# Attention's value products in two bursts of eight per head, with eight exponential buffers

## What is computed

```python
scores = einsum('bhqd,bhkd->bhqk', q, k) * scale          # 16 heads of 16 features
sparsity = scores.max(-1) - scores.mean(-1)
_, top_idx = top_k(sparsity, U)                             # U = 307 queries of 2048 per head
q_sel = take_along_axis(q, top_idx[..., None], axis=2)
attn = softmax(einsum('bhud,bhkd->bhuk', q_sel, k) * scale)
out_sel = einsum('bhuk,bhkd->bhud', attn, v)
out = zeros_like(q).at[bi, hi, top_idx].set(out_sel)
```

## Time and profile before

| what | us |
|---|---|
| median of 3 runs | 1661.31 (1660.96 to 1672.83) |
| the profiled execution's own time | 1666.39 |
| its span | 1664.6 |
| PE busy in the span | 1508.7 (91%) |
| DVE busy | 1225.6 (74%) |
| ACT busy | 1043.5 (63%) |
| granted TensorE clock, mean | 0.979 |

### The profile page before, as it was taken

How to read it: one execution, slowest core, us unless ns; L and a number is a source line. 1 busy time by engine, 2 the same in 40 slices (tenths; PEclk the granted TensorE clock), 3 DMA queues, 4 the chain that set the end, 5 groups by cost and what they waited for, 6 DMA issues and landing times.

```text
span 1664.6 us, 28574 instructions
## 1 busy us (share of the span) xinstructions
PE 1508.7 (91%) x8669; PEld 843.6 (51%) x8674; DVE 1225.6 (74%) x2906; ACT 1043.5 (63%) x1401; POOL 274.9 (17%) x321
## 2 busy tenths in 40 slices
PE   6799999998889979999998889989899999989999
PEld 3342222223445532222222645544698987479988
DVE  5569999998887749999999887856755452665511
ACT  4478888887756658888887446663333473333364
POOL 2340000001623343000000313341111000011100
PEclk9899999999999999999999999999999999999999
DMA  4662111211521121111112211111043402004410
GB/s 158 208 193 53 41 38 38 53 51 49 161 87 52 51 60 38 38 46 49 38 38 89 63 34 49 53 52 36 17 142 122 139 29 76 0 26 161 161 48 32
DMA packets 93336, 119.31 MB, mean 72 GB/s; under 512 B 22754, under 2 KB 78658, under 8 KB 92740
## 3 DMA queue, kind: packets, MB, share of 16 engines
q1 hardware_dynamic: 90180, 117.60, 23.3%
q0 software_dynamic: 3072, 0.66, 0.4%
HBM read 93.41 MB, written 24.78 MB: 71 GB/s over the span
## 4 chain that ended last, share of the span: by engine, by line
PE 45%; DVE 34%; issue 13%; DMA 4%; ACT 3%; SPq 1%; POOL 0%; DVEq 0%; ACTq 0%
DVE work_area L1208 24%; PE psum L2070 6%; PE psum L2008 6%; PE psum L1855 5%; PE psum L1876 5%; PE psum L1867 4%; PE psum L1951 4%; PE psum L2019 3%; DVE big_area L1208 2%; PE psum L2028 2%; DMA work_area<-heads_out 2%; PE psum L1691 2%; PE psum L2060 1%; PE psum L1716 1%; ACT big_area L891 1%
## 5 line engine op out<-in xcount | busy, mean ns | idle before, releaser
L1208 DVE CUSTOM_DVE_ANT_0 work_area<-psum,work_area 128x1024 f32<-128x1024 f32 x512 | 589.0, 1220 | 7.9 <-PE psum L1752 4.3
L820 ACT ACTIVATE work_area<-psum 128x1024 f32<-128x1024 f32 x512 | 511.0, 1027 | 75.7 <-DVE big_area L1208 30.1
L1752 PE MATMUL psum<-work_area 96*128 96x512 bf16 x1024 | 309.3, 384 | 47.9 <-DVE big_area L1208 6.8
L1742 PE MATMUL psum<-work_area 96*128 96x512 bf16 x1024 | 305.5, 380 | 7.4 <-ACT work_area L820 1.5
L838 ACT ACTIVATE work_area<-psum 128x614 f32<-128x614 f32 x256 | 164.1, 681 | 90.3 <-PE psum L1867 90.1
L1752 PEld LDWEIGHTS psum<-work_area 96*128 96x128 bf16 x1024 | 63.4, 97 | 266.3 <-DVE big_area L1208 251.2
L1742 PEld LDWEIGHTS psum<-work_area 96*128 96x128 bf16 x1024 | 88.8, 98 | 152.9 <-ACT work_area L820 59.0
L674 POOL DMA_INDIRECT heads_out<-work_area x96 | 98.3, 1024 | 193.8 <-DVE work_area L1374 172.7
L1352 DVE TENSOR_SCALAR big_area<-iota,rank 128x308 bf16<-128x308 f16 x512 | 119.0, 309 | 0.1
L2008 PE MATMUL psum<-work_area,xn 128*128 128x128 f32 x1024 | 118.5, 277 | 0.0
L2008 PEld LDWEIGHTS psum<-work_area,xn 128*128 128x128 f32 x1024 | 117.2, 194 | 0.2
(11 more groups left out here) (252 smaller groups left out, 1973.4 us busy)
## 6 DMA issues: line engine op xcount, KB each, us to landing
work_area<-in_L_ffn_w_dram SPq DMA_DIRECT2D x32, 1024.0 KB, 5.4
work_area<-k_parts SPq DMA_DIRECT2D x192, 64.2 KB, 2.2
work_area<-q_parts SPq DMA_DIRECT2D x192, 64.0 KB, 2.1
k_parts<-work_area SPq DMA_DIRECT2D x24, 384.0 KB, 4.1
q_parts<-work_area SPq DMA_DIRECT2D x16, 384.0 KB, 3.3
big_area<-q_parts SPq DMA_DIRECT2D x16, 384.0 KB, 5.5
work_area<-k_parts SPq DMA_DIRECT2D x32, 192.0 KB
x_res<-in_L_attn_x_dram SPq DMA_DIRECT2D x8, 512.0 KB, 5.7
```

The costliest lines, as they stand in the source:

```text
L820: s.activation(SC[:, t % 4], PS[:, 2 * (n % 2):2 * (n % 2) + 2].rearrange("p a n -> p (a n)"), ACT.Relu).then_inc(relu_done, 1)
L1208: v.tensor_tensor_reduce(SC[:, t % 4], PS[:, 4 + 2 * (t % 2):6 + 2 * (t % 2)].rearrange("p a n -> p (a n)"), SC[:, t % 4], 1.0, -3.0e38, A ...
L1742: last = mm(PS[:, 2 * (n % 2) + k], QS1[par][0:TERMS, t * P:(t + 1) * P], KS[par][0:TERMS, k * 512:(k + 1) * 512], start=True, stop=True)
L1752: last = mm(PS[:, 4 + 2 * (t % 2) + k], QS1[par][0:TERMS, t * P:(t + 1) * P], KS[par][0:TERMS, K1 + k * 512:K1 + (k + 1) * 512], start=Tru ...
```

## The change

PX grows from four to eight buffers (one for each pair of key tiles), five in the work area and three in EO. The two that overlap the busy area are now the last two, 6 and 7. The value products come in two bursts of eight key tiles. `pe_head` has a new order: scores 2, 3; the last 8 gathers of head h+1; rows(h); scores 4, 5; values 0; scores 6, 7; the first 8 gathers of head h+2; turn(h-1); then `k2_used`; scores 0, 1 of head h+1; values 1. Head 0 has all 16 gathers of head 1 after values 0, and head 1 has all 16 of head 2 after scores 2, 3. On ACT the copy of the next queries moves from behind exponential 6 to behind exponential 3 (head 0: behind 5), the wait for `parts_ready` moves ahead of exponential 6, and a wait for `zero_out` is added. DVE's order is unchanged; take_out waits for two bursts in place of four.

```diff
         OS = a.take([CH * P])
         QS = a.take([2, UP], BF16)
         SK = a.take([2, NT, TERMS + 6], BF16)
-        PX = a.take([4, 2, UP])
+        PX = [a.take([2, UP]) for _ in range(3)]
         OR = a.take([CH, DH + 1])
         ORr = a.take([CH])
         ON = a.take([2, CH, DH])
         IDX = a.take([2, CH], U32)
+        PX += [a.take([2, UP]) for _ in range(2)]
         attention_end = a.at
+        EO = sb("expert_out", [P, E, D])
+        zeros = EO[:].rearrange("p e d -> p (e d)")
+        a = Area(zeros)
+        for k in range(3):
+            PX.insert(3 + k, a.take([2, UP]))
         a = Area(work, L // 2)
         MK = a.take([2, NT * H], BF16)
...
         E2 = a.take([2, M])
         E2T = a.take([2, E, P])
         Y = a.take([2, D])
-        EO = sb("expert_out", [P, E, D])
-        zeros = EO[:].rearrange("p e d -> p (e d)")
         cmc = sb("slot_max_col", [P, E])
         warm = sb("exp_warm", [P, 1])
         nrm, z2, rz2 = (sb(n, [P, NT]) for n in ("nrm", "z2", "rz2"))
...
                     for k in gs:
                         v = i * 16 + (par * 8 + k)
                         act.wait_ge(s_ready, b * 128 + v + 1)
-                        act.wait_ge(p_used, b * 64 + i * 8 + (par * 4 + k // 2 + 1))
-                        slot = k % 4
-                        s.activation(PX[:, slot, :, 0:U], PS[:, 2 * (k % 2):2 * (k % 2) + 2, 0:U], ACT.Exp, scale=SCALE).then_inc(p_ready, 1)
-
+                        act.wait_ge(p_used, b * 32 + i * 4 + par * 2 + k // 4 + 1)
+                        s.activation(PX[k][:, :, 0:U], PS[:, 2 * (k % 2):2 * (k % 2) + 2, 0:U], ACT.Exp, scale=SCALE).then_inc(p_ready, 1)
+
+                act.wait_ge(zero_out, 64)
                 take_queries(0, 0, 0)
                 if b == 0:
                     second_part(1, NU - 1)
                 def act_head(i, par, more):
-                    if b == 0 and i == 0 and par == 0:
-                        exps(i, par, range(0, 3))
-                        act.wait_ge(parts_ready, B * NU)
-                    exps(i, par, range(3 if b == 0 and i == 0 and par == 0 else 0, 7))
+                    first = i == 0 and par == 0
+                    exps(i, par, range(0, 6 if first else 4))
                     if more:
                         take_queries(i, 1 - par, par + 1)
-                    exps(i, par, range(7, 8))
+                    if first and b == 0:
+                        act.wait_ge(parts_ready, B * NU)
+                    exps(i, par, range(6 if first else 4, 8))
                 for h in range(H):
                     act_head(h // 2, h % 2, h < H - 1)
...
                     v.tensor_scalar(IDX[:, par], PS[:, 7, CH * P:CH * P + CH], hcol[:, bass.ds(i * 2 + n, 1)], None, ALU.add).then_inc(idx_used, 1)
                 def take_out(i, par):
-                    dve.wait_ge(p_used, b * 64 + i * 8 + ((par + 1) * 4 + 2))
+                    dve.wait_ge(p_used, b * 32 + i * 4 + (par * 2 + 4))
                     v.tensor_copy(OS[:, 0:U], PS[:, 6 - par, 0:U]).then_inc(os_ready, 1)
                 def finish(i, par, n):
...
                         last = mm(PS[:, 2 * (k % 2) + kk, 0:U], K2S[n % 2][0:TERMS + 3, kt * P:(kt + 1) * P], QS[0:TERMS + 3, n % 2, 0:U], start=True, stop=True)
                     last.then_inc(s_ready, 1)
-                def values(i, n, k4):
-                    if k4 == 0:
+                def values(i, n, half):
+                    if half == 0:
                         pe.wait_ge(oT_used, max(0, b * H + i * 2 + n - 1))
-                    pe.wait_ge(p_ready, b * 128 + i * 16 + (n * 8 + 2 * k4 + 4))
-                    for q in range(4):
-                        kt = 4 * k4 + q
-                        last = mm(PS[32 * q:32 * q + DH + 1, 6 - n % 2, 0:U], V[:, kt, i * 2 + n], PX[:, kt // 2 % 4, kt % 2, 0:U], start=(kt < 4), stop=(kt >= NT - 4), skip_group_check=True)
+                    pe.wait_ge(p_ready, b * 128 + i * 16 + (n * 8 + 4 * half + 6))
+                    for kt in range(half * (NT // 2), (half + 1) * (NT // 2)):
+                        at = 32 * (kt % 4)
+                        last = mm(PS[at:at + DH + 1, 6 - n % 2, 0:U], V[:, kt, i * 2 + n], PX[kt // 2][:, kt % 2, 0:U], start=(kt < 4), stop=(kt >= NT - 4), skip_group_check=True)
                     last.then_inc(p_used, 1)
                 def rows(i, n):
...
                     last.then_inc(oT_ready, 1)
-                def pe_head(i, n, first, later):
-                    CUTS = (0, 0, NT // 2, NT) if first else (0, 5, 11, NT)
-                    for k4 in range(3):
-                        scores(i, n, 2 * k4 + 2)
-                        scores(i, n, 2 * k4 + 3)
-                        values(i, n, k4)
-                        if k4 < 2 and later > 0:
-                            gather(i, n + 1, range(CUTS[k4 + 1], CUTS[k4 + 2]))
-                        if k4 == 2:
-                            if first and b == 1:
-                                pe.wait_ge(x1_done, NT + 2)
-                            rows(i, n)
-                            if not first:
-                                turn(i, n - 1)
+                def pe_head(i, n, later):
+                    first, second = i == 0 and n == 0, i == 0 and n == 1
+                    for k in (2, 3):
+                        scores(i, n, k)
+                    if later > 0 and not first:
+                        gather(i, n + 1, range(0 if second else NT // 2, NT))
+                    if first and b == 1:
+                        pe.wait_ge(x1_done, NT + 2)
+                    rows(i, n)
+                    for k in (4, 5):
+                        scores(i, n, k)
+                    values(i, n, 0)
+                    if first:
+                        gather(i, n + 1, range(NT))
+                    for k in (6, 7):
+                        scores(i, n, k)
+                    if later > 1 and not first:
+                        gather(i, n + 2, range(NT // 2))
+                    if not first:
+                        turn(i, n - 1)
                     pe.wait_ge(s_ready, b * 128 + i * 16 + (n * 8 + 8))
                     pe.sem_inc(k2_used, 1)
                     for k in range(2):
                         if later > 0:
                             scores(i, n + 1, k)
-                    values(i, n, 3)
-                    if later > 1:
-                        gather(i, n + 2, range(0, 5))
+                    values(i, n, 1)
                 gather(0, 0, range(NT), True)
                 scores(0, 0, 0)
...
                 pe.wait_ge(v_done, NT * (b + 1))
                 pe.wait_ge(v_ones, 1)
                 for h in range(H):
-                    pe_head(h // 2, h % 2, h == 0, min(2, H - 1 - h))
+                    pe_head(h // 2, h % 2, min(2, H - 1 - h))
                 turn(PAIRS - 1, 1)
```

## The result

The changed kernel takes 1692.72 us (median of 4 runs, 1690.50 to 1695.34) against 1665.43 for the kernel before beside it (4 runs, 1660.96 to 1672.83): ratio 1.0146, 95% interval 1.0117 to 1.0175, so slower by 1.5%. (The plain quotient of the two medians is 1.0164, inside that interval.) The forecast was 1690. The profiled execution took 1690.5, its span is 1688.7 against 1664.6, and its mean granted clock 0.978 against 0.979.

The account below looks back on a forecast made before the run. PE was taken to set attend's pace at 7.90 us a head, until the new order closes a loop through DVE. Loop terms 5.6 + 11.9, small parts 1.5 and clock falls 9.3 add 28.3 to 1661.3: about 1690 us, range 1672 to 1704.

Parts of the forecast that it names:

- The ring: Closed PE-DVE loop through take-out, one-hots, gathers and value burst, once a head: 8.48 us in attend(0), 9.30 in attend(1).
- The sum over the heads: Thirteen loop periods a batch: attend(0) 110.2 against 104.67, +5.6 us; attend(1) 120.4 against 108.47, +11.9.
- The clock: PE clock falls after idle time in attend(1): five of eleven heads at 1.85 us each, 9.3 us; none in attend(0).
- long head 3: Head 3 of attend(1) has the roots in its chain, so its loop period is 10.45 us.
- The small parts: Head 0's later first value products and the last burst of each batch: 0.8 us a batch, 1.5 for both.
- its wait for the keys: PE in head 15 of batch 0 keeps its 5.58 us of idle time for the key load.
- The total: Whole kernel: 19.0 + 9.3 = 28.3 us slower, median from 1661.3 to about 1690.
- (a): The loop as predicted in both batches, but the clock holds at full: 1680 us; chance 0.26.
- (b): The clock falls in every head of attend(1) from 3 on: 19.0 + 20.4, 1701 us; chance 0.12.
- (d): One-hots hidden, PE then key load sets the pace near 7.75 us in every head: 1655 us; chance 0.06.
- (e): Bursts of eight gain nothing (1.30 us each): 3.4 us above the forecast; 0.46 together with the forecast.
- (c): The loop is shorter by 0.3 us in each of 26 heads, without falls: 1672.5 us; chance 0.08.

Follow-up runs that it names:

- e3: Changed kernel with take-out of a head moved behind the one-hots on DVE; 1685.40 us, ratio 0.9993.
- e4: Changed kernel with one unneeded DVE reduction of 0.59 us ahead of build in each head; 1709.20 us, ratio 1.0131.
- e5: Kernel before with the same added DVE reduction per head as in e4; 1669.85 us, ratio 1.0013.
- second pair: Kernel before and changed kernel, both unedited, run and profiled once more on one chip; 1669.19 and 1691.31 us, ratio 1.0152.
- second group: Runs on a chip where the kernel before takes 1668.99 us: e5, the second pair and e8.
- e8: Kernel before with a head's key load in six DMAs of 16 rows in place of three of 48, 32 and 16; 1659.74 us, ratio 0.9949.
- groups 1, 3 and 4: Sets of follow-up runs on other chips, where the unedited kernel before takes 1686.03, 1684.77 and 1688.30 us.
- e1: Changed kernel with the first eight gathers of head h+2 moved back behind the last value burst; 1710.23 us, ratio 1.0138.
- e9: Changed kernel with the six key DMAs of e8; 1690.93 us, ratio 1.0026.
- e11: Changed kernel with e3's edit, six key DMAs, and the second norm's two steps moved behind one-hots and take-out; 1682.19 us, ratio 0.9985.
- e12: The kernel of e11 run once more, against the kernel before at 1688.30 us; 1689.32 us, ratio 1.0004.
- e7: The changed kernel, unedited, run once more beside the kernel before; 1691.31 us, ratio 1.0152.

## Why the prediction was right, step by step

**The ring: right, in place and size.** Its terms in attend(1), from the rows above: take-out to the end of the one-hots 5.76 (5.84 predicted), to the gathers 0.06 (0.07), gathers 1.10 (1.09), turn 0.32 (0.38), scores 0, 1 0.62 (0.62), burst to take-out 1.30 (1.30): 9.16 for 9.30. In attend(0) ordinary heads take 8.3 to 8.5, on the mean 8.42 over thirteen (8.48 predicted), with 0.80 to 1.01 us idle in each (0.85 predicted). That the wait is a ring and not only a late engine is shown by e3 (broken at DVE: 15 us gone from attend(1)) and e4 with e5 (of 0.59 us of DVE work 0.54 counts in one order and none in an undisturbed head of the other).

**The sum over the heads: right for attend(0), +4.8 (+6.0 in the second pair) for +5.6.** In attend(1) it was 120.4 without falls; 122.7 and 121.1 were measured with two and one.

**The clock: the term that was mis-sized.** The forecast let five of eleven heads fall, at 1.85 each, 9.3 us. In the profile after two fell, and in the second pair one. Windows of the changed kernel (columns as in the earlier trace rows), in the long head 3, in the middle of the loop, and after the gathers of head 13:

```profile
1021.00:1024.00 3.00, 3.00 (x22) 0.95 (x19) 0.89 (x4) 1.25 (x2) 0.98 (x1) 0.50 0.26 66
1052.00:1060.00 8.00, 6.36 (x58) 4.26 (x62) 6.20 (x28) 4.84 (x10) 3.41 (x3) 1.00 0.16 48
1113.00:1116.00 3.00, 3.00 (x14) 2.40 (x13) 0.43 (x2) 0.00 (x0) 0.00 (x0) 0.52 0.09 19
```

PE idled 2.71 us ahead of the first of them (the long chain of head 3) and 1.70 ahead of the last; the nine heads between them idled 1.54 to 1.70 and kept 1.00, 2.4 GHz, as in the second row; the falls are to 0.50, 1.2 GHz. So the length of one idle time does not decide; the rows of before, one fall in two, were too few to count by. A fall costs 1.35 to 1.65 us (head 3: 11.8 and 12.1 for 10.45, which is the forecast's figure, since no head 3 without a fall was seen; head 13: 10.8 for 9.2), and 1.5 to 1.6 in e4, so 1.85 was a little high. With falls at 3.0 us in place of 9.3 the thirteen heads come to 17.5 + 3.0 = +20.5, where +19.0 was measured. The two rules of "TensorE: Matmul & The Clock Gate" in the Trainium skill stand on either side of this: by the section "HAM oscillation" no idle time of the ring is long enough for a fall, and two heads fell; by "A second HAM failure mode: psum-queue depth-cycling" most heads of attend(1) should have swung, and nine of eleven did not. The prediction called the gap of the first rule longer than any here, but its own have one: 5.58 us ahead of head 15 of batch 0, with the granted clock at 0.50 from 604 to 608, and here the trace agrees with the rule.

**The small parts: right in sum.** Head 0 of both batches together came to +0.9 and heads 14, 15 to +0.6, 1.5 together as predicted; in the second pair they came to +2.9 and +0.7, so the exact 1.5 is luck. But head 15 of batch 0 did not keep its wait for the keys. PE's timeline of the changed kernel:

```profile
609.91 1.19 PE L1871 MATMUL psum<-work_area 99*128 99x307 bf16 x4 [8.22 <-DMA work_area<-k_parts]
```

It grew from 5.58 to 8.22. From the issue of this load to the end of what PE can do without it there were 9.3 us of PE's time before (588.75 to 598.05) and 7.5 now (594.22 to 601.69), and the load itself, with the 24 other DMAs that SP issues behind it, took 15.6 us for 14.8. In the second pair the wait grew only from 7.35 to 7.74. What heads 14 and 15 save on PE went there.

**The total.** In the profiled spans 28.3 us were predicted and 24.1 came. The thirteen heads gave 7.8 less (19.0 for 26.8): 6.3 of it from the falls, 1.5 from a ring shorter by 0.1 us a head. Outside them it was 3.6 more (5.1 for 1.5), all of it outside attention's heads, where I can name no part of the change, and 2.4 of it ahead of the first scores. The medians moved by 27.3, in the second group by 22.3. So the ring was right; the count of the falls was not, and that 1690 was met so closely is in part luck, because time outside the heads and the spread between executions made up for it. In the second pair the spans are 1667.5 and 1686.5, +19.0; that this is rival (a)'s figure is luck too, for the two stages of attention grew by 24.7 there and the rest of the kernel shrank by 5.6. But the mechanism, the ring with hardly a fall, is nearer to (a), which should have had the larger chance.

**The rivals.** (b) is out: the clock did not fall in every head. (d) is out by the 30.1 us of waits in the thirteen heads. (e) is out by the burst of 1.16. (c), a shorter ring, holds only for 0.1 us a head. Of (d) one part was true: the key load does limit the kernel before, by 9 us (e8), though nearly all of it in the last two heads of batch 0 and not, as (d) had it, in each head.

## What to carry to other kernels

When an order written by hand is changed, look for the ring that it closes: follow each wait of the moved step back through the other engine's own order, to see whether it needs something that now stands behind it. A ring can't catch up, its length is the time of a round whatever the busy shares say, and the cheap repair may lie at the other end, here one copy of 0.48 us moved. And where an engine idles briefly before the consumer of a load, try the load's shape before the order: six even DMAs in place of three uneven ones gave 0.5% in the kernel before, which no order did.

## What the runs showed of the hardware

- **Late signals of PE.** On the chips of groups 1, 3 and 4 semaphore events of scores, most often of scores 2 and 3, and in e1, e3, e9, e11 and e12 of the gathers behind them too, come up to 2.6 us after the ends of those matmuls (1.9 to 2.5 in most heads of e1's attend(0)), bunched, mostly 0.4 to 1.3 us after the end of a scatter on POOL. They go with up to 25 us of idle time in attend(0) and 13.5 in attend(1). In the six profiles of group 2 and of the first comparison, where the kernel before is 16 to 23 us faster, all 256 such events of the scores are recorded and none is over 0.01 us behind its matmul's end; in each of the eight others at least 19 are over 1 us late, and 5 to 39 are missing from the record. The changed kernel was clean there (e7), and with only a probe added it has them on the chip of group 1 (e4), so they seem to go with the chip. That is argued, not shown: the kernel before and the changed one have no profile on those chips. Why a scatter should hold PE's signals stays open; a kernel without the scatter wasn't tried.
- **The clock and short idle times.** The same idle time, 1.54 to 1.70 us once a head, is followed by a fall in one head and not in nine.
- **The shape of a load:** the same 96 rows of keys arrive in 8.1 to 9.5 us by three DMAs (before) and in 4.3 to 6.1 by six (e8); where 24 other DMAs are issued behind them, in 14.8 by three and in 4.45 by six.
